# Weighing half of the heads of an attention with rounded halves of probabilities and keys in place of full-precision products

## The reference

```
x = x + tanh(g_xattn) * attention(layernorm(x), ctx_512)      # 16 heads of 64
x = x + tanh(g_ffn)   * experts(layernorm(x))                 # 32 experts, 8 taken per token, and a shared MLP

attention: scores = (q Wq)(kv Wk)^T * 64**-0.5 per head; attn = softmax(scores); out = (attn (kv Wv)) Wo + bo
experts:   sigmoid gate, the best 2 of 4 groups, the best 8 experts in them; out = sum of weight * down(silu(gate(x)) * up(x))
```

## Time and profile before

| | |
|---|---|
| median of 3 runs | 669.35 us (668.38 to 670.52) |
| the profiled execution | 671.43 us, its span in the trace 669.6 us |
| PE busy | 654.7 us (98%) |
| DVE busy | 499.4 us (75%) |
| ACT busy | 366.1 us (55%) |
| POOL busy | 286.0 us (43%) |
| granted TensorE clock | 1.0 in all of the span |

### The profile page before, as it was taken

The page is one execution under the profiler, slowest core; times in us unless marked ns, Lnnn a source line. Parts: engine busy times, 40 slices in busy tenths (PEclk is TensorE's granted clock), DMA queues, the critical chain, the costliest instruction groups (busy, mean ns, idle before and its releaser), DMA issues.

```text
span 669.6 us, 13644 instructions
## 1 busy us (share of the span) xinstructions
PE 654.7 (98%) x3676; PEld 473.9 (71%) x3676; DVE 499.4 (75%) x1330; ACT 366.1 (55%) x689; POOL 286.0 (43%) x317
## 2 busy tenths in 40 slices
PE   8998999999999999999998999999999999999997
PEld 5665666666666666666656878788787878888785
DVE  5879767767677676776786978969596877869564
ACT  3464555555555555565455555555655555555553
POOL 4123222232323323233210755656565666656554
PEclk9999999999999999999999999999999999999999
DMA  7313332332323323232224735264654536364550
GB/s 187 95 49 83 75 81 62 79 91 64 77 63 79 84 70 77 61 82 77 63 71 128 163 86 138 82 159 110 137 135 101 132 77 156 84 158 111 139 132 16
DMA packets 63244, 65.58 MB, mean 98 GB/s; under 512 B 26080, under 2 KB 41568, under 8 KB 63200
## 3 DMA queue, kind: packets, MB, share of 16 engines
q1 hardware_dynamic: 63200, 65.07, 39.4%
HBM read 61.64 MB, written 2.88 MB: 96 GB/s over the span
## 4 chain that ended last, share of the span: by engine, by line
PE 64%; issue 9%; POOL 8%; DMA 8%; DVE 5%; SPq 4%; ACT 1%; DVEq 0%; POOLq 0%; ACTq 0%
PE bank L1119 12%; PE bank L1120 12%; PE bank L1121 12%; PE bank L1195 9%; POOL halves L500 8%; PE bank L1219 5%; DMA inverse_bc<-inverse_dram 4%; PE bank L1155 3%; PE bank L1175 2%; DMA inverse_dram<-inverse 2%; PE bank L1234 2%; SPq L292 2%; PE bank L1184 1%; PE bank L1178 1%; PE bank L1181 1%
## 5 line engine op out<-in xcount | busy, mean ns | idle before, releaser
L500 POOL TENSOR_TENSOR halves<-area,halves 128x512 fp32r<-128x512 f32 x135 | 175.3, 1299 | 141.5 <-ACT halves L628 135.5
L641 ACT ACTIVATE area<-bank 128x512 f32<-128x512 f32 x136 | 81.4, 599 | 112.3 <-PE bank L1121 111.3
L581 ACT ACTIVATE area<-bank 128x512 f32<-128x512 f32 x128 | 69.5, 595 | 120.6 <-PE bank L1184 120.6
L1079 DVE TENSOR_TENSOR bank<-area,bank 128x512 f32<-128x512 f32 x128 | 88.7, 693 | 52.8 <-PE bank L1121 52.7
L1195 PE MATMUL bank<-area,ctx_keys 128*65 128x512 f32 (+1 forms) x256 | 124.7, 599 | 0.9 <-ACT u_odd L534 0.9
L1119 PE MATMUL bank<-x2t_hi,w_hi 128*128 128x512 f32 x272 | 110.1, 405 | 0.1
L1120 PE MATMUL bank<-x2t_hi,w_lo 128*128 128x512 f32 x272 | 107.1, 394 | 0.0
L1121 PE MATMUL bank<-x2t_lo,w_hi 128*128 128x512 f32 x272 | 106.3, 391 | 0.0
L446 POOL TENSOR_TENSOR ctx_hi<-ctx_raw,ones_col 128x128 fp32r<-128x128 f32 x32 | 18.4, 576 | 202.0 <-DMA ctx_raw<-ctx_t 202.0
L770 DVE TENSOR_REDUCE row_max<-bank 128x4 f32<-128x512 f32 x128 | 81.7, 680 | 26.1 <-PE bank L1155 22.5
L628 ACT ACTIVATE halves<-area 128x512 fp32r<-128x512 f32 x136 | 85.1, 626 | 16.9 <-DVE area L1087 16.4
(11 more groups left out here) (128 smaller groups left out, 1095.8 us busy)
## 6 DMA issues: line engine op xcount, KB each, us to landing
wbc<-rows_dram SPq DMA_DIRECT2D x128, 256.0 KB, 4.3
inverse_bc<-inverse_dram SPq DMA_DIRECT2D x64, 256.0 KB, 3.9
w_raw<-experts SPq DMA_DIRECT2D x32, 102.0 KB, 2.0
ctx_raw<-ctx_t SPq DMA_DIRECT2D x32, 64.0 KB, 1.9
ctx_keys<-ctx_nat SPq DMA_DIRECT2D x32, 64.0 KB, 2.1
out<-area SPq DMA_DIRECT2D x7, 256.0 KB, 4.0
max_rows<-max_t SPq DMA_DIRECT2D x64, 4.0 KB
area<-wq_t SPq DMA_DIRECT2D x1, 512.0 KB, 4.4
```

Source lines behind the costliest of these rows:

```text
L500: nc.gpsimd.tensor_tensor(hid_lo[:, u % SLOTS, :], hid[:, u % HIDS, :], raw(hid_hi[:, u % SLOTS, :]), ALU.subtract).then_inc(hidlo_ready, 1)
L581: nc.scalar.activation(probs_t[:, k, :, :], st_ps[q][:].rearrange("p (h n) -> p h n", h=4), ACT.Exp)\
L641: nc.scalar.activation(silu_g[:, u % 2, :], gate_ps[u % 2][:], ACT.Silu).then_inc(silu_ready, 1)
L1079: nc.vector.tensor_tensor(up_ps[u % UPS][:], silu_g[:, u % 2, :], up_ps[u % UPS][:], ALU.mult)\
```

## The change

The products of h 1 (`weigh` with h = 1) of every batch are replaced by `weigh_halves`. Probabilities and keys are split: ACT copies the two probability tiles of h 1 into a rounded high half (`probs_high`, two activations 128x512), DVE subtracts it from the probabilities for the low half (`probs_low`, two subtractions 128x512), and POOL splits the batch's keys in the same way (`split_keys`, two operations 128x192). PE then makes six rounded products in place of two full ones: for each q high keys x high probabilities and low keys x high probabilities, and after both q, high keys x low probabilities for each q. The halves live in buffers that are free at the time (`x2t_hi`, `x2t_lo`, the tail of the expert weights' halves, and in the last chunk `a_hi` and `a_lo`). h 0 is weighed as before.

The diff's core:

```diff
--- before.py
+++ after.py
...
+        p_hi = [x[:, 1, :] for x in (x2t_hi, x2t_lo)]
+        tail = slice(WCOLS - 2 * 3 * CD, WCOLS)
+        p_lo_at = ([x[:, 0, :] for x in (x2t_hi, x2t_lo)], [x[:, 0:4, :].rearrange("p h n -> p (h n)") for x in (a_hi, a_lo)])
+        keys_at = ([w[:, tail].rearrange("p (s n) -> p s n", s=2) for w in (w_hi, w_lo)],
+                   [x[:, 4:7, :].rearrange("p h n -> p (h n)").rearrange("p (s n) -> p s n", s=2) for x in (a_hi, a_lo)])
...
         st_done, exp_ready = sem("st_done"), sem("exp_ready")
+        phi_ready, plo_ready = sem("phi_ready"), sem("plo_ready")
+        keyshi_ready, keyslo_ready = sem("keyshi_ready"), sem("keyslo_ready")
         u_done, u_ready, inverse_ready = sem("u_done"), sem("u_ready"), sem("inverse_ready")
...
+            def split_keys(b, t, c, last):
+                keys_hi, keys_lo = keys_at[last]
+                if last:
+                    pool.wait_ge(g_done, 8 * NCH)
+                pool.wait_ge(keys_in[b], 16 * c + 16)
+                wait(pool, u_done, 4 * (t - 1))
+                nc.gpsimd.tensor_tensor(keys_hi[:, b % 2, :], ctx_keys[:, b, :], ones_col[:].broadcast_to([P, 3 * CD]),
+                                        ALU.mult).then_inc(keyshi_ready, 1)
+                pool.wait_ge(keyshi_ready, t + 1)
+                nc.gpsimd.tensor_tensor(keys_lo[:, b % 2, :], ctx_keys[:, b, :], raw(keys_hi[:, b % 2, :]), ALU.subtract)\
+                    .then_inc(keyslo_ready, 1)
...
                     t = CB * c + b
+                    split_keys(b, t, c, last)
                     split_weights(b % 2, t, 2 * c + b // 2, NB if last else t + CB)
...
+            def probs_high(t):
+                act.wait_ge(exp_ready, 4 * t + 4)
+                for q in range(2):
+                    nc.scalar.activation(p_hi[q], probs_t[:, 2 + q, :, :].rearrange("p h n -> p (h n)"), ACT.Copy)\
+                        .then_inc(phi_ready, 1)
...
                     if last and b == 1:
+                        act.wait_ge(u_done, 4 * (NB - CB))
                         x2t_high(0, 0)
...
                         sigmoid_high(0, ut_ps)
+                    if b % 2 == 0 or last:
+                        probs_high(t)
                     u_out(t, b % 2, 0, 0)
...
                     u_out(t, b % 2, 0, 1)
+                    if b % 2 == 1 and not last:
+                        probs_high(t)
                     if last and b == 0:
...
+            def probs_low(t, last):
+                for q in range(2):
+                    dve.wait_ge(phi_ready, 2 * t + q + 1)
+                    nc.vector.tensor_tensor(p_lo_at[last][q], probs_t[:, 2 + q, :, :].rearrange("p h n -> p (h n)"),
+                                            raw(p_hi[q]), ALU.subtract).then_inc(plo_ready, 1)
...
                                 route_chunk_0(*SEAM[step_of_chunk])
+                        if h == 1:
+                            probs_low(t, last)
                         if h == 0 and not (first and b < 2):
...
+            def weigh_halves(t, b, last):
+                keys_hi, keys_lo = keys_at[last]
+                pe.wait_ge(keyslo_ready, t + 1)
+                for q in range(2):
+                    pe.wait_ge(phi_ready, 2 * t + q + 1)
+                    wait(pe, u_ready, 4 * t + q + 1)
+                    cols = slice(0, CD + 1) if q == 0 else slice(CD, 3 * CD)
+                    ps = u_ps[q][0:CD + 1 if q == 0 else P, :]
+                    nc.tensor.matmul(ps, keys_hi[:, b % 2, cols], p_hi[q], start=True, stop=False)
+                    nc.tensor.matmul(ps, keys_lo[:, b % 2, cols], p_hi[q], start=False, stop=False)
+                for q in range(2):
+                    pe.wait_ge(plo_ready, 2 * t + q + 1)
+                    cols = slice(0, CD + 1) if q == 0 else slice(CD, 3 * CD)
+                    nc.tensor.matmul(u_ps[q][0:CD + 1 if q == 0 else P, :], keys_hi[:, b % 2, cols], p_lo_at[last][q],
+                                     start=False, stop=True).then_inc(u_done, 1)
...
                     if started:
-                        for q in range(2):
-                            weigh(t - 1, (b - 1) % CB, 1, q, c + (b > 0))
+                        weigh_halves(t - 1, (b - 1) % CB, last and b > 0)
                     if b == 1 and not last:
...
             in_chunks(pe, attention)
-            for q in range(2):
-                weigh(NB - 1, CB - 1, 1, q, NCH)
+            weigh_halves(NB - 1, CB - 1, True)
             transpose_weights(0, y_ps)
```

## The result

The changed kernel takes 686.1 us (median of 4 runs, 684.62 to 686.18) against 668.87 us beside it on the same chip: ratio 1.0249 [1.0231, 1.0267], 17.2 us slower by the medians and 16.7 by the ratio. The forecast was 675.7, with 665 to 681 as its range. The sign is right and the time lies 5 us outside the range. The profiled execution of after took 684.62 us with a span of 682.8, 13.2 more than the profiled one of before.

The account below looks back on a forecast made before the run. The bound was taken to be a two-batch ring of 20.68 us through row maxima, scores and the inverses' DMAs, not PE. Steady part 0, start 1.3 and last chunk 5.0 gave 6.3 us slower: 675.7 us, range 665 to 681.

Parts of the forecast that it names:

- PE's saving: PE, products of h 1: six rounded products save 0.34 us per batch, taken as 0 gain in the steady part.
- The steady part: Loop rounds: the added ACT and DVE work fits in waits or is hidden, PE's saving gains nothing; 0 us.
- The start: Batches 2 and 3: probs_low on DVE lacks cover and delays normalise and take_max; 0.7 to 1.9, taken as 1.3 us.
- The last chunk: Last chunk, where DVE also carries the routing: probs_low stands in its way four times, 5.0 us in sum.
- (a): Last chunk: probs_low(27) on gapless DVE delays the inverse of 27 and the normalise waiting for it, +1.24 us.
- (b): Last chunk: probs_low(29) ahead of the routing's first level delays ACT, SP and the sums of batch 29, +1.24 us.
- (c): Last chunk: probs_low(30) stands between 344.13 and 351.27, where DVE has no idle mark, +1.24 us.
- (d): Last chunk: probs_low(31) behind the routing's end holds PE's last two products and transpose_weights, +1.24 us.
- Rival A: Steady part: PE is the bound, so its saving counts, -9.5 us, ending at 666.2 us; chance 0.17.
- Rival C: Loop: new operations meet and lengthen the ring, normalise by 0.35 us in 13 rounds, 4.6 us, 680.3; chance 0.09.
- Rival D: Seam before the experts: PE's clock slows through low activity, 3.2 us more, 678.9 us; chance 0.08.

Follow-up runs that it names:

- one_product: Changed kernel with only the high keys x high probabilities product left, without probs_low and the keys' low half: 673.7 us, ratio 1.0051.
- steady_low_first: Changed kernel with halves for batches 3 to 27 only and probs_low ahead of ln_apply at the first batch of a chunk: 672.8 us, ratio 1.0069.
- start_only: Changed kernel with halves for batches 0 to 2 only, the others weighed as before: 672.51 us, ratio 1.0057.
- end_only: Changed kernel with halves for batches 28 to 31 only, the others weighed as before: 674.72 us, ratio 1.0089.
- keys_once: Changed kernel without POOL's splitting of the keys of batches 2 to 27, which use stale halves: 683.71 us, ratio 1.0205.
- end_low30: end_only with probs_low of batch 30 ahead of the routing pieces on DVE: 675.62 us, ratio 1.0101.
- end_busy: end_only with four unread products into a free bank in PE's waits around the third products of batches 30 and 31: 677.39 us, ratio 1.0099.
- end_quiet: end_only with POOL's split of batch 29's keys held until DVE has written the layer norm's xn before the experts: 673.5 us, ratio 1.0066.

## Why the prediction was wrong

Its terms against the runs:

- **PE's saving** (0.34 us a batch, worth nothing): right. The rounded products stand 0.23 us apart, and one_product shows no gain even from 1.26 us a batch. Rival A, given 0.17, is out.
- **The steady part** (0): this is the step that failed, in the sentence "In a steady round the two pairs stand behind `residual`, off the ring". It had been read off the round of batches 15 to 17, with 3.78 and 2.50 us of waiting on DVE. At the first batch of a chunk `ln_apply` stands between `residual` and `probs_low`, and "what is queued behind them" was asked, but not when PE itself wants them. Measured: 9.0 us for batches 3 to 27, 4.3 to 4.5 of them by that order alone. Of the other 4.6, left in steady_low_first, its profile has 1.7 up to batch 7; the rest is in what the profiles don't resolve.
- **The start** (1.3 for batches 2 and 3): 3.8 us for batches 0 to 2 by start_only, and batch 3 comes on top. The mechanism was right, DVE has no cover but the 0.58 us; the size was off. At the reciprocal of batch 2 the lag is 1.5 us, where 0.66 was forecast: the pair took 1.87 us beside POOL's operations and not 1.24, and 0.15 came from batch 1's pair. By batch 7 it is 2.4 us; where the other 1.4 are lost, one profile doesn't tell.
- **The last chunk** (5.0): 6.0 us by end_only, without batch 27. The size was nearly right, by luck: only one of the four terms came out. (a) is made up again. (b) shows 0.2 us at the reciprocal of batch 29; ahead of it `normalise` had waited 1.19 us for the inverses before, and doesn't wait in end_only. (c) is 1.2, as forecast. (d) is 3.1 us instead of 1.24, the clock in it. Not on the list were the layer norm's steps stretched beside POOL (1.6 us at batch 27).
- **Rival C** (contention, 0.35 a round) looked only at `normalise`. keys_once puts the splitting of the keys of batches 2 to 27 at 3 us, and the rows that are longer are those of DVE's other operations.
- **Rival D** said that no row shows a fall of the clock later on. After has such rows, with a granted clock of 0.50, that is 1.2 GHz instead of 2.4:

```profile
54.00:56.00 2.00, 0.79 (x3) 1.00 0.35 121
56.00:58.00 2.00, 1.72 (x10) 0.75 0.55 150
58.00:60.00 2.00, 2.00 (x11) 0.50 0.09 12
60.00:62.00 2.00, 2.00 (x17) 0.90 0.39 105
```

  But the fall costs nothing there: start_only, with the same products, keeps 1.00 through these microseconds, and its reciprocal of batch 2 starts at 62.54 where that of after starts at 62.53. At the end of the last chunk it is part of the 3.1 us by the rows of end_low30, but end_busy won nothing from keeping it up.

What is open: most of 4.6 us of the loop's 9.0, 1.4 us of the start, and why end_busy lost in the experts what it gained ahead of them.

## What to carry to other kernels

For an operation added to an engine "in its slack", look at every different round of the schedule, first and last chunk and the odd stage inside the loop included, and ask at each not only who is queued behind it but when its own consumer wants it. A new wait on a lightly loaded engine moves that engine's old work as well, and may move it beside work that it slows. Busy 98% is no proof of a bound: here work saved on the busiest engine was worth nothing, and half a microsecond in the order of the DMA queue was worth more than all of it.

## What the runs showed of the hardware that I had not expected

- Small DVE steps with two inputs in SBUF took 0.38 to 0.49 us in place of 0.18 beside POOL operations on SBUF (end_only), a subtraction of 128x512 up to 1.11 in place of 0.68 (after). Which of the two engines is held up changes from place to place: in end_quiet POOL's split of a 128x192 tile took 1.33 us beside a `normalise` of 1.21, and 0.51 in end_only while DVE's steps were the longer ones.
- The granted clock of PE fell to 0.50 in the middle of a kernel, after 2 us in which PE was busy for 0.79 of them (start), and to a mean of 0.60 in 360 to 364 us after four microseconds with 2.04 of PE busy (last chunk of after). In end_busy four products into an unused bank kept it at 1.00, without a gain.
